# A graph network layer on one core: the decoder's rows are added first, not last, in VectorE's step

## What is computed

```
h     = x @ w_lin + b_lin
dense = h[edge_src], placed at [edge_dst, slot < 32]          mask = slot is filled
xb    = mab(dense, dense, enc, mask)                          32 x 32 attention in each node
xp    = relu(xb @ pma_lin_w + pma_lin_b)
p     = mab(pma_seed, xp, pma, mask)                          one query pools the 32 slots
dd    = mab(p, p, dec)                                        the decoder, one row for each node
out   = layernorm(x + relu(nan_to_num(dd)))
mab(x, y): softmax(q k^T / 8) v @ out_w + out_b + x = h;  h + relu(h @ ff_w + ff_b)
```

## Time and profile before

| | |
|---|---|
| median of 3 runs | 4447.55 us |
| the profiled execution: time, span | 4459.52 us, 4457.7 us |
| busy: TensorE, VectorE, ScalarE, GpSimd | 73%, 68%, 37%, 69% of the span |
| DMA | 368.55 MB, 83 GB/s |
| mean granted clock of TensorE | 0.845 |

### The profile page before, as it was taken

One profiled execution on the slowest core, in us unless ns is written; L12 is line 12 of the kernel. 1 busy time (PEld: TensorE's weight loads), 2 busy tenths in 40 slices (PEclk: granted clock), 3 DMA queues, 4 the chain that ended last, 5 costly groups with the idle time before them and its releaser, 6 DMA issues.

```text
span 4457.7 us, 87178 instructions
## 1 busy us (share of the span) xinstructions
PE 3270.3 (73%) x30724; PEld 2035.1 (46%) x30724; DVE 3038.5 (68%) x7088; ACT 1656.4 (37%) x2990; POOL 3060.7 (69%) x3236
## 2 busy tenths in 40 slices
PE   4777777777777777777777676777776767777777
PEld 3444444444444444444444454544444545444444
DVE  5667676767666667676666676766666667666776
ACT  2334333433333334343333343433333333333433
POOL 3777776767677667676676676766766767667771
PEclk7888888888888888888888888888888888888888
DMA  5333332222222222222232222222222222222330
GB/s 192 84 87 87 85 87 81 81 81 82 78 80 82 78 79 81 78 82 79 78 83 77 82 79 78 82 81 79 82 78 82 78 78 82 78 80 81 90 96 19
DMA packets 170667, 368.55 MB, mean 83 GB/s; under 512 B 56189, under 2 KB 109093, under 8 KB 170229
## 3 DMA queue, kind: packets, MB, share of 16 engines
q0 software_dynamic: 158032, 342.73, 27.9%
q1 hardware_dynamic: 11877, 19.76, 1.2%
q10 hardware_dynamic: 320, 0.10, 0.0%
HBM read 349.58 MB, written 16.32 MB: 82 GB/s over the span
## 4 chain that ended last, share of the span: by engine, by line
PE 47%; DVE 27%; issue 20%; POOL 4%; DVEq 1%; ACT 0%; DMA 0%; SPq 0%; ACTq 0%; POOLq 0%
PE ps L695 10%; PE ps L722 6%; PE ps L637 6%; PE ps L738 5%; PE ps L649 5%; DVE windows L951 5%; PE ps L681 4%; PE ps L708 4%; POOL gathered L545 4%; DVE xb L1090 3%; DVE h L1060 3%; DVE top L1097 2%; DVE total L1047 2%; PE ps L673 2%; DVE flags L906 2%
## 5 line engine op out<-in xcount | busy, mean ns | idle before, releaser
L545 POOL DMA_INDIRECT gathered<-node_table,idx x3125 | 2963.1, 948 | 1217.7 <-issue 894.1
L695 PE MATMUL ps<-h,ff_diag 128*128 128x512 f32 x782 | 506.1, 734 | 551.7 <-DVE h L1060 551.7
L759 ACT ACTIVATE h_apart<-ps 64x512 f32<-64x512 f32 x782 | 462.2, 591 | 989.3 <-PE ps L637 979.7
L1090 DVE SCALAR_TENSOR_TENSOR xb<-ps,cols,h 128x512 f32<-128x512 f32 x391 | 293.7, 751 | 671.9 <-PE ps L695 671.9
L637 PEld LDWEIGHTS ps<-ident,gathered 128*128 128x128 f32 x3128 | 481.2, 203 | 395.5 <-issue 395.5
L637 PE MATMUL ps<-ident,gathered 128*128 128x128 f32 x3128 | 575.3, 312 | 66.2 <-DMA gathered<-node_table,idx 66.1
L1171 DVE STREAM_TRANSPOSE probs_diag<-probs 32x512 f32<-32x512 f32 x784 | 548.9, 700 | 18.3
L722 PE MATMUL ps<-xb,pma_diag 128*128 128x512 f32 x782 | 524.5, 758 | 26.8 <-DVE xb L1090 20.6
L649 PE MATMUL ps<-probs_diag,gathered 128*64 128x128 f32 x6256 | 457.6, 290 | 91.2 <-issue 85.7
L649 PEld LDWEIGHTS ps<-probs_diag,gathered 128*64 128x64 f32 x6256 | 370.2, 169 | 264.6 <-issue 242.6
L814 ACT ACTIVATE xp<-ps,cols 128x512 f32<-128x512 f32 x391 | 267.2, 683 | 513.3 <-PE ps L722 513.2
(11 more groups left out here) (195 smaller groups left out, 3564.1 us busy)
## 6 DMA issues: line engine op xcount, KB each, us to landing
gathered<-node_table,idx POOLq DMA_INDIRECT x3125
node_table<-gathered SPq DMA_DIRECT2D x24, 384.0 KB, 2.6
out_rows<-rows SPq DMA_DIRECT2D x5, 416.0 KB
win_table<-in_dst SPq DMA_DIRECT2D x1, 1716.0 KB
win_table<-in_src SPq DMA_DIRECT2D x1, 1716.0 KB
windows<-win_table,win_idx POOLq DMA_INDIRECT x94
rows<-in_x SPq DMA_DIRECT2D x2, 640.0 KB, 5.2
rows<-in_x SPq DMA_DIRECT2D x1, 768.0 KB, 7.1
```

The source lines that it names most:

```text
L545: pool.indirect_dma_start(out=gathered[:, s.slot(0, RING), t * ROW:(t + 1) * ROW], out_offset=None, in_=table, in_offset=bass.IndirectOffs ...
L695: pe.matmul(ps[:, B_FF, :], ff_diag[:, :], h2[:, s.slot(L_FF, 2), :], start=True, stop=True).then_inc(ff_ps, 1)
L759: return nc.scalar.activation(o, i, ACT.Copy)
L1090: V.scalar_tensor_tensor(xb[:, s.slot(L_FF, 2), :], ps[:, B_FF, :], c_("ff_b", P), h2[:, s.slot(L_FF, 2), :], ALU.add, ALU.max).then_inc(x ...
```

## The change

`y_rows` is cut in two. The add, with its wait for `fin_ps`, becomes the first thing in VectorE's step 3, ahead of the end of the softmax. The statistics stay where both stood, behind the transposes, with their wait for `y_ok`. Nothing is added or left out, and no other engine's code changes.

```
             def step(s):
+                if s.has_iteration(L_Y):
+                    y_rows(s)
                 if s.has_batch(L_SOFTMAX):
...
                     to_diagonal(s, pr, 0, QUADS)
                 if s.has_iteration(L_Y):
-                    y_rows(s)
+                    y_stats(s)
...
                 V.scalar_tensor_tensor(row, ps_fin[:, 0:D], nonempty[:, bass.ds(m, 1)], row, ALU.mult, ALU.add
                                        ).then_inc(y_ok, 1)
+
+            def y_stats(s):
+                m = s.iteration(L_Y)
+                row = rows[:, bass.ds(m, 1), :].rearrange("p m d -> p (m d)")
                 dve.wait_ge(y_ok, m + 1)
                 V.bn_stats(stats[:, bass.ds(m, 1), :].rearrange("p m n -> p (m n)"), row).then_inc(stats_ok, 1)
```

## The result

The changed kernel takes 4171.15 us (median of 4 runs, 4164.36 to 4172.48), the kernel before 4448.81 us (4 runs). The ratio is 0.9366, 95% interval 0.9343 to 0.9389: 6.3% faster. The prediction was 4168 us in a range of 4150 to 4225, and 0.95 on faster. The profiled execution took 4171.78 us, its span is 4170.0 us.

The account below looks back on a forecast made before the run. The TensorE-VectorE loop bounds the kernel before. Gains of 2.85 and 1.4 us make 4.25 per iteration, above GpSimd's 3.4 of room, so the time was summed on GpSimd's queue: span 4165.7 plus 1.8, 4168 us, range 4150 to 4225.

Parts of the forecast that it names:

- The gap and its releaser: TensorE before L708: the add behind VectorE's transposes holds the pooling matmuls through y_ok; moving it saves 3.17 us per iteration.
- Rival D: Before L708: something ending with the transposes, not y_ok, holds the pooling matmuls; gap stays, about 4490 us; chance 0.03.
- GpSimd as the new bound: GpSimd's 32 gathers and one window fetch per iteration, 41.35 us, become the limit: 4168 us; chance 0.67.
- the sum on its queue: GpSimd's last gather, from 4365.76, gets back 266.4 us of waits for TensorE and starts at 4099.4; span 4165.7 us.
- the tail: From octet 390's transposition to the end: 66.75 us before, less 3.7 of one pooling gap, so 63.0 us.
- the room under 44.72: Per iteration, 44.72 us less GpSimd's own 41.35: 3.4 us can be gained before GpSimd becomes the bound.
- The 12 us: Median of the runs before lay 12 us below the profiled one; left out of the number, given to the range.
- Rival B: TensorE and VectorE stay the bound because the clock gives nothing back: 2.85 us per iteration, 4188 us; chance 0.20.
- The clock: TensorE's L722 and L738: without the gap the clock rises earlier, 1.4 us more per iteration, bounds 0 and 2.0.
- the sum of 2.85: Per iteration: 3.17 us of gap removed before L708 less 0.32 us for the add at the head.
- rival C: More TensorE idling, before L695 or for gathers, lowers its clock and loses 1.02 us per iteration: about 4284 us; chance 0.10.
- The cost at the head: VectorE's add in front of h2 costs 0.32 us per iteration in full; L695's wait for h grows about 0.3 us.

Follow-up runs that it names:

- the filled one: The kernel before, add still behind the transposes, with two idle matmuls in TensorE's gap before the pooling matmuls, in the loop only: 4253.54 us against 4441.26, ratio 0.9579.
- The four reduces: The changed kernel with four idle VectorE reduces of 128x512, 0.68 us each, at the head of each step that has output rows: 4278.98 us.

## Why the prediction was right, point by point

**The gap and its releaser: right.** The gap before L708 fell from 305.5 us to 0.4, and the pooling matmuls start directly behind the transposition. Rival D (something else holds them) is out.

**GpSimd as the new bound: right, and the sum on its queue held.** The last gather was put at 4099.4, the transposition of octet 390 at 4102.7, the tail at 63.0 us. In the trace of the changed kernel:

```profile
4100.08 0.95 POOL L545 DMA_INDIRECT gathered<-node_table,idx  x1 [0.30 <-issue]
...
4106.19 0.72 PE L637 MATMUL ps<-ident,gathered 128*128 128x128 f32 x4
```

The tail is 4170.0 - 4106.19 = 63.8 us. The 4.3 us by which the span exceeds the forecast 4165.7 are 0.7 in the last gather, 2.8 in TensorE, which did not wait there and came to octet 390 that much later than a waiting TensorE would, and 0.8 in the tail. One number on the way was wrong and cost nothing: the earlier trace rows give 1.256 us for a gather, and 33 x 1.256 = 41.45 us, not 41.35, so the room under 44.72 was 3.3 us by them, not 3.4. The time was summed on the queue and not from this pace. The 12 us by which the median before lay under its profiled execution did not carry over: the median after is within 1 us of its profiled one. Rival B is out, since GpSimd's 50 waits are 0.3 us each.

**The clock: the right mechanism; the size came out by luck.** The term "1.4 us, bounds 0 and 2.0" took the delay of the clock's rise, 6.0 us after unbroken work, from the stretch behind the gap, and so left L708 at the low level. In the changed kernel the rise came some 4 us after L695's start, inside the pooling matmuls. What the three groups took over the whole run, in the kernel before, the changed one and the filled one (matmuls, busy us, mean ns, idle before them):

```profile
L722 PE MATMUL ps<-xb,pma_diag 128*128 128x512 f32 x782 | 524.5, 758 | 26.8 <-DVE xb L1090 20.6
L738 PE MATMUL ps<-h_apart,qT 128*32 128x64 f32 x12544 | 262.2, 246 | 1.4 <-ACT h_apart L759 1.4
L708 PE MATMUL ps<-xp_rows,weights 128*32 128x512 f32 x784 | 188.2, 1048 | 306.0 <-issue 305.5 <-DVE rows L1193 0.4
```

```profile
L722 PE MATMUL ps<-xb,pma_diag 128*128 128x512 f32 x782 | 455.5, 665 | 27.3 <-DVE xb L1092 21.1
L738 PE MATMUL ps<-h_apart,qT 128*32 128x64 f32 x12544 | 221.0, 222 | 1.5 <-ACT h_apart L759 1.4
L708 PE MATMUL ps<-xp_rows,weights 128*32 128x512 f32 x784 | 159.5, 898 | 0.4 <-DVE rows L1195 0.4
```

```profile
L726 PE MATMUL ps<-xb,pma_diag 128*128 128x512 f32 x782 | 446.4, 653 | 26.4 <-DVE xb L1094 20.1
L742 PE MATMUL ps<-h_apart,qT 128*32 128x64 f32 x12544 | 222.4, 223 | 1.4 <-ACT h_apart L763 1.4
L712 PE MATMUL ps<-xp_rows,weights 128*32 128x512 f32 x784 | 111.9, 639 | 115.8 <-issue 115.4 <-DVE rows L1197 0.4
```

From 974.9 to 836.0 us is 138.9 us, 1.4 for each of the 98 iterations: the forecast's number. But its parts were wrong and made up for each other: L708 gave 0.3 us (nothing was forecast), L722 0.7 (0.45) and L738 0.4 (0.97, since over the run it was less often at the low level than in the step that was read). The filled gap gives 974.9 - 780.7 = 194.2 us in its 88 iterations, 2.2 each, above the upper bound of 2.0, in which L708 was taken to be low in any case; there it mostly ran at the high level. None of this reached the time: any term above 0.6 us lifts the sum of 2.85 over GpSimd's 3.4. The four reduces put the uncapped gain at 44.72 - 39.95 = 4.8 us, an estimate; the 0.5 us by which it exceeds 4.25 are not accounted for.

The Trainium skill's rule ("TensorE: Matmul & The Clock Gate", "What's actually happening"), that activity releases the throttle, is borne out by the fill in its plainest form: nothing released earlier, no work of use added, and matmuls at nearly twice the speed (L712: 1.06 us in place of 1.94). Its "HAM oscillation" section was weighed as the mechanism of rival C. Waits for gathers did come, 485.3 us, 3.02 us long in the step shown and followed by a low clock; but the mean granted clock rose to 0.901, and the groups behind such waits, L637 and L695, took 588.6 and 509.9 us in the whole run against 575.3 and 506.1 before. That is 17 us more, where C wanted 1.02 x 94 = 96, and GpSimd's pace covered it.

**The cost at the head: its sign in the profile wrong, its size not shown.** I said the wait of L695 for `h` would grow by 0.3 us each. It fell from 551.7 to 255.5 us, since TensorE now comes to that point later itself, held by the gather in front of it. Moving the add on to between `h2` and `xb` took 49.5 us of that wait away, but no time. The term of 0.32 us, called the part that rests on no estimate, is seen in the time of no run: with all gathers GpSimd's pace covers it, and with seven the place of the add made no difference.

## What to carry to other kernels

A semaphore is raised when the instruction that carries it runs, so what stands in front of a tiny instruction on its own engine can become a wait on another (here 2.89 us of transposes before an add of 0.28 us): ask for each release whether its input was ready long before, and put it ahead of work that nobody else needs. Before adding up what a shorter loop brings, work out the next engine's own pace per iteration (here 33 x 1.256 us, from a stretch in which it never waited); the gain ends there, and a dummy load on the engine that is no longer the bound measures the distance. An idle gap of TensorE cost this kernel its length and, behind it, matmuls at half speed; filling the gap tells the two apart.

## What the runs showed that I had not expected

Two idle matmuls in a gap of 3.2 us, 88 times, made the kernel before 4.2% faster (4441.26 to 4253.54 us); TensorE's busy time hardly changed for it (3260.7 us with them, 3270.3 without), since what they added the others saved.

In the two groups with one gather fewer, the kernel before, with all its gathers, took 5561 to 5619 us, where the other groups gave 4441 to 4449. It was not profiled there; in the traces of the kernels with seven gathers TensorE stopped 477 to 717 times among matmuls with no wait between them. All runs of such a group were slow alike, so ratios within a group stand, and comparisons across groups do not. There, leaving out one gather in eight made the kernel before 6% faster (5561.5 to 5228.8 us), although GpSimd waited for TensorE for 1164.8 us in the faster of the two; whether the gathers and the supply of instructions share something was not tried.
